# A Mamba-2 block on one core: decay matrices in steps of 64 tokens in place of 128

## The reference, cut to what matters

```python
proj = einsum('bsd,ed->bse', x, in_proj_w)          # gate | hBC | dt
hBC = silu(conv4(hBC))                              # hs | B | C
dt = clip(softplus(dt + dt_bias), 0, 100);  A = -exp(A_log)
xch = hs * dt                                       # in chunks of 128 tokens
A_cum = cumsum(dt * A)                              # in each chunk
L = exp(segsum(dt * A))                             # 128 x 128, lower triangle
Y_diag = einsum('lhn,shn,hls,shp->lhp', C, B, L, xch)
states = einsum('lhn,hl,lhp->hpn', B, exp(A_cum[-1] - A_cum), xch)
Y_off = einsum('lhn,hpn,hl->lhp', C, prev_states, exp(A_cum))
y = Y_diag + Y_off + hs * D;  g = y * silu(gate)
out = rmsnorm_per_group(g) * norm_w @ out_proj_w.T
```

## Time and profile before

| | |
|---|---|
| median of 3 runs | 1868.56 us (1868.19 to 1874.12) |
| profiled execution | 1870.32 us, span 1868.5 us |
| PE busy | 1754.7 us, 94% |
| PE weight loads | 1344.0 us, 72% |
| DVE busy | 1290.5 us, 69% |
| ACT busy | 1065.5 us, 57% |
| POOL busy | 942.1 us, 50% |
| mean granted TensorE clock | 0.988 |
| a group of four units | 216.9 us |

### The profile page before, as it was taken

The page is one execution under the profiler, slowest core; times in us unless marked ns, Lnnn a source line. Parts: engine busy times, 40 slices in busy tenths (PEclk is TensorE's granted clock), DMA queues, the critical chain, the costliest instruction groups (busy, mean ns, idle before and its releaser), DMA issues.

```text
span 1868.5 us, 31134 instructions
## 1 busy us (share of the span) xinstructions
PE 1754.7 (94%) x9656; PEld 1344.0 (72%) x9656; DVE 1290.5 (69%) x2095; ACT 1065.5 (57%) x1946; POOL 942.1 (50%) x721
## 2 busy tenths in 40 slices
PE   6799999999999999999999999999999999999966
PEld 5567777777777777777777777777777777777755
DVE  5766667666766677766676667666777666766788
ACT  6566555656646565665546566465656555565632
POOL 2355453556535464554535555355644545455563
PEclk9899999999999999999999999999999999999988
DMA  6412121111202121121211212121211212111121
GB/s 224 130 30 69 55 66 44 50 60 57 66 28 72 49 66 51 35 66 55 66 45 48 62 54 68 29 72 45 70 51 29 72 55 66 44 48 61 34 96 57
DMA packets 77097, 114.14 MB, mean 61 GB/s; under 512 B 21376, under 2 KB 28032, under 8 KB 76032
## 3 DMA queue, kind: packets, MB, share of 16 engines
q1 hardware_dynamic: 59360, 80.06, 14.2%
q10 hardware_dynamic: 17568, 31.99, 5.1%
HBM read 88.94 MB, written 23.07 MB: 60 GB/s over the span
## 4 chain that ended last, share of the span: by engine, by line
issue 46%; POOL 34%; PE 9%; DVE 5%; ACT 3%; DMA 1%; SPq 1%; POOLq 1%; ACTq 0%; DVEq 0%
POOL yt L1605 9%; POOL ssq L1600 7%; POOL wg_lo L1524 4%; POOL wo_lo L1524 4%; POOL prev L1586 3%; POOL yt L1608 3%; POOL wx_lo L1524 3%; PE bank L476 2%; PE bank L478 2%; PE bank L477 2%; PE bank L641 1%; PE bank L706 1%; DMA raw_w<-w_in_dram 1%; PE bank L840 1%; ACT lm L1072 0%
## 5 line engine op out<-in xcount | busy, mean ns | idle before, releaser
L1605 POOL TENSOR_TENSOR yt<-yt,ea 128x384 f32<-128x384 f32 (+1 forms) x128 | 189.6, 1481 | 393.1 <-DVE ea L1440 393.1
L1218 DVE SCALAR_TENSOR_TENSOR xc<-bank,bpar,xc 128x511 f32<-128x511 f32 (+2 forms) x384 | 285.4, 743 | 52.8 <-ACT xc L906 48.3
L1410 DVE TENSOR_TENSOR lm<-lm,cbm 128x512 f32<-128x512 f32 x256 | 185.9, 767 | 155.7 <-ACT lm L1075 155.7
L476 PE MATMUL bank<-h_hi,wg_hi 128*128 128x512 f32 x640 | 262.0, 409 | 31.3 <-ACT gate L1030 21.9
L478 PE MATMUL bank<-h_hi,wg_lo 128*128 128x512 f32 x640 | 251.0, 392 | 0.0
L477 PE MATMUL bank<-h_lo,wg_hi 128*128 128x512 f32 x640 | 250.2, 391 | 0.0
L476 PE MATMUL bank<-wo_hi,g_hi 128*128 128x512 f32 x496 | 206.9, 417 | 7.2 <-POOL wo_lo L1524 7.2
L476 PE MATMUL bank<-h_hi,wx_hi 128*128 128x512 f32 x512 | 210.3, 411 | 2.2 <-DVE bt L1218 2.2
L1586 POOL TENSOR_TENSOR prev<-prev,dec 128x512 f32<-128x512 f32 x96 | 102.0, 1063 | 206.0 <-DVE prev L1356 131.9
L478 PE MATMUL bank<-h_hi,wx_lo 128*128 128x512 f32 x512 | 200.3, 391 | 0.0
L477 PE MATMUL bank<-h_lo,wx_hi 128*128 128x512 f32 x512 | 199.9, 390 | 0.0
(11 more groups left out here) (187 smaller groups left out, 3796.9 us busy)
## 6 DMA issues: line engine op xcount, KB each, us to landing
raw_w<-w_in_dram SPq DMA_DIRECT2D x145, 256.0 KB, 2.6
raw_w<-w_out_dram SPq DMA_DIRECT2D x64, 256.0 KB, 2.6
part_d<-part ACTq DMA_DIRECT2D x64, 256.0 KB, 2.0
part<-part_d ACTq DMA_DIRECT2D x58, 256.0 KB, 2.7
rt<-rows_d SPq DMA_DIRECT2D x256, 8.0 KB
acc<-x_dram SPq DMA_DIRECT2D x8, 256.0 KB, 6.6
acc<-w_mod_dram SPq DMA_DIRECT2D x2, 1024.0 KB, 6.0
lh<-neg_d SPq DMA_DIRECT2D x128, 8.0 KB
```

The source lines that it names most:

```text
L476: nc.tensor.matmul(out_ap, whi(k), hhi(k), start=(k == 0), stop=False)
L1218: stt(dst[:, at], ps[:, 0:HALF - 3 + k], w(k), dst[:, at], ALU.mult, ALU.add)\
L1410: tt(lm[:, h % 4, :], lm[:, h % 4, :], cbm[:, toks(hf)], ALU.mult).then_inc(v_m, 1)
L1605: tt(yt[:, j % 2, cols], yt[:, j % 2, cols], ea[:, j % 2, cols], ALU.add).then_inc(p_t3, 1)
```

## The change

Steps of 64 tokens (`SUB`), two to a chunk of 128, for everything that has a decay in it.

- Differences, decays and mix: the matrix of a head is now 64 by 64 for each of 8 sub-chunks, packed with the even sub-chunks of a half on rows 0 to 63 and the odd ones on rows 64 to 127, two heads side by side in 512 columns. `diff(j)` is two products of 256 columns into bank 2; ACT has one Relu and one Exp a step for two, DVE one multiply for two. `lm` has two buffers for four.
- Y_diag: for each chunk four products of 64 rows, 64 weight columns and 64 columns, (head, sub-chunk) = (0, 0), (1, 1), (1, 0), (0, 1), with the two sub-chunks in two banks (3 and 5). The pass over `yt` is split in two. A semaphore increment of its own, `t_open`, stands ahead of them.
- Y_off: one matmul of 64 columns for each sub-chunk, k from 1 in even units.
- States: `states(z)` makes two products of 64 rows, into banks 6 and 7 (in odd units the last has one). 8 adds and 7 decays in an even unit, 7 and 7 in an odd one, for 4 and 3, and 3 and 3. `xw` is made for all four z in odd units too.
- Order on PE in the first part: `states(z-1)` follows the transposes of z and precedes the large product; in z = 3 come `states(2)`, `exp_a(0)`, `diff(0)`, `out_proj(2)`, `states(3)`, `out_proj(3)`. The waits for the last accumulate's variance and for B's transposes move to `states(0)`.
- Order on POOL: the group's rstd, decay 0, the splits of z = 0 and 1, decays 1 and 2, the splits of z = 2, the other decays, the splits of z = 3.
- Parameters: 12 DMAs into `rt`, 4 into `lh`, one into `dec`.
- Prologue: the sum restarts every 64 tokens (`seg`); one DVE pass and one exponential replace the 8 exponentials.

```diff
                 def states(z):
-                    te.wait_ge(v_xw, sb0 + z + 1)
...
+                    te.wait_ge(v_xw, 4 * u + z + 1)
...
                     else:
-                        te.wait_ge(v_prev, sb0 + z)
-                    nc.tensor.matmul(bank[7][:, :], bt[:, toks(hf, z, 1)], xw[:, z % 2, :],
-                                     start=True, stop=True).then_inc(t_st, 1)
+                        te.wait_ge(v_prev, ab0 + 2 * z)
+                    for s in range(1 if hf == 1 and z == NZ - 1 else 2):
+                        lst = nc.tensor.matmul(bank[6 + s][:, :], bt[sub_rows(s), toks(hf, z, 1)],
+                                               xw[sub_rows(s), z % 2, :], start=True, stop=True)
+                    lst.then_inc(t_st, 1)
...
+                def diff(j):
...
+                        te.wait_ge(a_fall, 4 * u + j)
+                    for i in range(2):
+                        lst = nc.tensor.matmul(bank[2][:, i * NZ * SUB:(i + 1) * NZ * SUB],
+                                               lh[par_][32 * j:32 * j + SROWS, i * 128:(i + 1) * 128],
+                                               rt[par_][32 * j:32 * j + SROWS, 0:NZ * SUB], start=True, stop=True)
+                    lst.then_inc(t_diff, 1)
...
+                    elif z == 1:
+                        ge(te, v_t2, 4 * u)
...
                 for z in range(NZ):
                     transposes(z)
+                    if z >= 1:
+                        states(z - 1)
                     if z == 2:
                         gate_proj(g, c, 3)
-                        states(1)
                         continue
                     if z == 3:
+                        exp_a(0)
+                        diff(0)
                         if not first and not end:
                             out_proj(u - 1, 2)
-                        states(2)
-                        exp_a(0)
-                        diff(0)
-                        diff(1)
+                        states(3)
...
-                    for z in range(1 - hf, NZ):
-                        lst = nc.tensor.matmul(bank[6][:, chunk(z)], prev[:, slot(hf, z), j * 128:(j + 1) * 128],
-                                               ct[:, toks(hf, z, 1)], start=True, stop=True)
+                    for k in range(1 - hf, NS):
+                        lst = nc.tensor.matmul(bank[6][:, k * SUB:(k + 1) * SUB],
+                                               prev[:, slot(k), j * 128:(j + 1) * 128],
+                                               ct[:, subtoks(hf, k)], start=True, stop=True)
                     lst.then_inc(t_yo, 1)
...
+                    te.sem_inc(t_open, 1)
                     for z in range(NZ):
-                        for i in range(2):
-                            h = 2 * j + i
-                            lst = nc.tensor.matmul(bank[5][64 * i:64 * i + 64, chunk(z)],
-                                                   xdt[:, z, h * HDIM:(h + 1) * HDIM], lm[:, h % 4, chunk(z)],
-                                                   start=True, stop=True)
+                        for i, s in ((0, 0), (1, 1), (1, 0), (0, 1)):
+                            h, at = 2 * j + i, (i * NZ + z) * SUB
+                            lst = nc.tensor.matmul(yd[64 * i:64 * i + 64, s, z * SUB:(z + 1) * SUB],
+                                                   xdt[sub_rows(s), z, h * HDIM:(h + 1) * HDIM],
+                                                   lm[sub_rows(s), j % 2, at:at + SUB], start=True, stop=True)
                     lst.then_inc(t_yd, 1)
...
+                def decay(k):
+
+                    if k == 1 - hf:
+                        po.wait_ge(d_par[hf], 272 * (nb + 1))
+                        ge(po, t_yo, 4 * u)
+                    po.wait_ge(v_prev, ab0 + k)
...
+                if not first and c in (0, 3):
+                    group_rstd(g - 1 if c == 0 else g, 1 if c == 0 else 0)
+                if hf == 1:
+                    decay(0)
+                for f in todo[0] + todo[1]:
+                    unit_fill(f, g)
+                decay(1)
+                decay(2)
+                for f in todo[2]:
+                    unit_fill(f, g)
+                for k in range(3, NS - hf):
+                    decay(k)
+                for f in todo[3]:
+                    unit_fill(f, g)
```

More of the change, by code:

```diff
@@ L47, in adaln_mamba_ffn @@
         xw = sb("xw", [128, 2, BLOCK])
[L48 to L49 removed]
+        prev = sb("prev", [128, NS, BLOCK])
+        lm = sb("lm", [128, 2, HALF])
         ea = sb("ea", [128, 2, HALF])
@@ L327, in _ @@
             xt = x.rearrange("(t p) n -> t p n", p=128)
-            mods = [flat(xdt, 0, 4), flat(gate, 0, 4), flat(prev, 0, 4), flat(lm, 0, 4), flat(acc, 0, 4), flat(acc, 4, 8)]
+            mods = [flat(xdt, 0, 4), flat(gate, 0, 4), flat(prev, 0, 4), flat(prev, 4, 8), flat(acc, 0, 4), flat(acc, 4, 8)]
             def load_mod(v):
@@ L501, in mod_row @@
                 te.wait_ge(d_mod[v], 16)
-                t, k0 = ((xdt, 0), (gate, 0), (prev, 0), (lm, 0), (acc, 0), (acc, 4))[v]
+                t, k0 = ((xdt, 0), (gate, 0), (prev, 0), (prev, 4), (acc, 0), (acc, 4))[v]
                 for k in range(NK):
@@ L679, in group_bc @@
                     for h2 in range(2):
[L680 to L683, removed]
+                        for k in range(NS):
+                            at = (h2 * NZ + k // 2) * SUB
+                            lst = nc.tensor.matmul(bank[2][sub_rows(k % 2), at:at + SUB], bt[:, subtoks(h2, k)],
+                                                   ct[:, subtoks(h2, k)], start=True, stop=True)
+                    lst.then_inc(t_cb, 1)
                     if first:
@@ L970, in _ @@
             keep_row(3)
-            se.wait_ge(v_scan, 2)
-            for z in range(NT):
-                lst = act(ea[:, z // 4, chunk(z % 4)], xw[:, z // 4, chunk(z % 4)], ACT.Exp, scale=-1.0,
-                          bias=xw[:, z // 4, (z % 4 + 1) * 128 - 1:(z % 4 + 1) * 128])
-            lst.then_inc(a_fe, 1)
+            se.wait_ge(v_drop, 1)
+            act(flat(ea, 0, 2), flat(ea, 0, 2), ACT.Exp).then_inc(a_fe, 1)
             pro_split(5)
@@ L1418, in lower_g @@
                         ALU.mult, ALU.subtract).then_inc(v_lo, 1)
+                new_state(5)
                 mix(0)
-                mix(1)
+                if not first and not end:
+                    accumulate(u, g1, b1, h1, 2)
+                new_state(6)
+                if hf == 0:
+                    new_state(7)
                 if not first and not end:
                     accumulate(u, g1, b1, h1, 3)
-                if hf == 0:
-                    new_state(3)
-                cols = slice(0 if hf else CHUNK, HALF)
+                cols = slice(0 if hf else SUB, HALF)
+                sub_first = lambda t: t.rearrange("p (z s l) -> p s z l", s=2, l=SUB)
                 for j in range(NCT):
                     if j < NCT - 1:
-                        mix(2 * j + 2)
-                        mix(2 * j + 3)
+                        mix(j + 1)
                     ve.wait_ge(t_yd, 4 * u + j + 1)
```

238 lines of the change are left out of this document (117 added, 121 removed).

## The result

The changed kernel takes 2053.2 us (median of 4 runs, 2049.8 to 2054.0) against 1870.7 for the kernel before in the same session: ratio 1.097, 95% interval 1.0945 to 1.0996, slower by 182.5 us. The forecast was 2192 us, with a range of 2040 to 2285. The direction and the range held; the likeliest case was 139 us too long, and rival A (2040 us) is the one that came nearest.

What follows compares the result with a forecast made beforehand. The prediction took PE, busy 94% of the span, as the bound; PE's added records, tiling changes, waits and clock loss, less waits taken back, summed to +323 us, giving 2192 us, range 2040 to 2285.

Steps and rivals of the forecast that it cites:

- rival A: PE quadrants wholly independent, both fp32 halves included: `xdt` by `lm` -55 us, state products +14; 2040 us, chance 0.16.
- B by C: On PE, once a group, 32 records with half the weight columns for 16; priced at nothing.
- Terms 2 and 3: On PE, partial overlap: `xdt` by `lm` on quadrants +49 us (0 to 97); state products on row groups +62 us.
- Term 1: `prev` by `ct` on PE: 8 more records a step, spacing set by weight load rather than columns: +102 us.
- Term 4: Changing PE's tiling in and out at each of four steps a unit: +40 us (0 to 52).
- Term 6: New PE waits before state pairs, for state adds behind POOL's decays and weight splits: +80 us (30 to 130).
- Rival C: State chain covered because a split or DMA comes earlier, so new waits and clock loss go: 2098 us, chance 0.06.
- Term 7: PE's clock falling after seven stalls of 6.4 us, 2 us each: +14 us (0 to 28).
- Term 8: PE waits taken back, for `ea`, the accumulate and half of the gate's: -24 us (0 to -40).
- Rival D: Faster: `prev` by `ct` records of 64 columns cost only their own 0.053 us; 1804 us, chance 0.04.
- B: No overlap over row groups on PE: `xdt` by `lm` +108 us, state products +110; 2294 us, chance 0.10.
- E: No difference: the saved decays pay for everything on ACT's side, if PE weren't the bound; chance 0.02.

Runs made afterwards that it cites:

- runs 3 and 4: Changed kernel with half the records of `prev` by `ct` (wrong results): one 128-column product per sub-chunk pair, 1982.9 us; the same list with 64 columns each, 1978.2 us.
- run 5: Changed kernel with one state product over all 128 rows in place of two over 64 rows (wrong states): 2036.4 us.
- Run 1: Changed kernel with decay 1 ahead of the weight splits on POOL, and later decays moved ahead likewise: 2013.2 us.
- runs 7 and 8: Run 1 with decays 3 and 5 ahead of splits, 2013.2 us; then the first accumulate behind the first state add in c = 0 and 3, 1993.1 us.
- run 2: Changed kernel with the sixteen `xdt` by `lm` products ordered one quadrant after another instead of in turns: 2154.3 us.
- run 6: Changed kernel, still 64-token steps, with PE's order of the kernel before, large product ahead of state products: 2074.7 us.

## Why the prediction was right in part

The sum again, with what the traces and runs show.

| term | forecast us | measured us | from |
|---|---|---|---|
| 1 `prev` by `ct` | +102 | +108 | 0.85 x 64 + 0.84 x 64 |
| 2 `xdt` by `lm` | +49 | -52 | (0.62 - 1.03) x 128 |
| 3 state products | +62 | +14 | 0.86 in 16 odd units |
| 4 changes of tiling | +40 | +46 | (3 x 0.18 + 0.09 + 4 x 0.20) x 32 |
| 6 new waits | +80 | +87 | 89.3 - 2.1 |
| 7 clock | +14 | +19 | 38 us of work at half clock |
| 8 taken back | -24 | -31 | rows 2 against the list above |
| B by C (in 5, at nothing) | 0 | -6 | (1.09 - 1.78) x 8 groups |
| sum | +323 | +185 | 182.5 measured |

**Terms 2 and 3 failed, by one assumption:** "again only neighbours of different products overlap, since a product's two records share a quadrant", and for the states "the second and third overlap and the others don't". The runs show whole products side by side: a pair of state products takes the time of one, and sixteen quadrant products stream in 0.6 of what eight took. I had rival A with just these values and gave it 0.16. In `xdt` by `lm` I took the middle between two bounds that both lay above the truth; the lower end there, no change, wasn't a bound, and A's -55 should have been it. The two terms came out 149 us below their forecast, the others 11 us above it together. The range held because its lower end had been set at A's sum, with 13 us to spare; term 2 itself had the wrong sign and lay outside its own bounds, so the range held by A and not by the mechanism that was forecast. The Trainium skill, "TensorEngine Tiling (Array Packing)", Key Properties, says that tiles work independently, weight loads and matmuls in parallel; the traces agree, 0.015 us a record with the quadrants in turns for 0.042 one after another.

**Term 1 held:** the one-column row of the trace before gave 0.10 us a record, eight more records cost 0.85 us, and runs 3 and 4 show that the columns have next to no part in it. (The 0.10 contains a short first distance; the single starts are 0.112 us apart at 1, 64 and 128 columns alike.) The sign given for it, 16 records in 1.6 to 1.8 us, was below the prediction's own sum, 1.08 + 0.8, and the measured 1.93. The same page of the Trainium skill, Instruction Overhead, gives a matmul about 60 cycles of overhead; by an estimate from that figure a record of 64 columns would cost half of one of 128, and this term nothing. No run agrees.

**Term 4** held in its sum, not in its parts: it took 0.09 us for going in everywhere, where behind the transposes it is 0.2, and run 5 puts the whole at 40 us for the state pairs.

**Term 6 held in its places as well as in its sum.** Forecast were 1.05 twice in c = 0, 1.7 in c = 1, nothing in c = 2, 6.4 and 0.95 in c = 3; the trace has 0.91 and 0.82, 1.51 and 0.29, nothing, 7.12 and nothing. Run 1 shows the cause that was named. What stays without the splits was mis-sized: 55 us of waits, where the prediction leaves 21 (7 x 0.95 and c = 0's share) and run 1's expectation 30, because the third split, the chain of adds and decays and DVE's accumulates are next (runs 7 and 8). Rival C falls with the wait of 7.1 us.

**Term 7** held, a little undersized. At each of the seven long waits the clock goes to half, for 6.8 or 10.2 us, and PE works in 4 to 6.5 us of it: 38 us in all, of which half is lost, 19 us.

**Term 8:** ACT's relief did reach PE's wait for the gate, 21.9 to 9.9 us, about the half that was taken.

Of the other signs DVE and POOL came near (1311 and 1093 us busy for 1300 and 1080). ACT was 954 us busy for 910, and PE's busy time grew by 136 us where its list was to grow by 230 to 260, which is terms 2 and 3 again.

Rival D, faster, fell with runs 3 and 4; B with the state pair, whose four records take what two take, and with run 2; E with the result.

## What to carry to other kernels

A short float32 product on TensorE (here up to 128 columns) with full 128 by 128 weights costs by its records, about 0.11 us each, and not by its columns: cutting 128 columns into two of 64 takes 1.93 us for 1.08, whatever the arithmetic saved. Cutting both dimensions onto quadrants is the other way round, as products on different quadrants run beside one another if they alternate in the list (0.62 us a step for 1.03). Each change into a row tiling and back costs, 0.3 us in run 5, so small groups must be kept together. When a serial chain gets more and shorter links, look in every queue on it for work that stood harmlessly between the old links, above all work that waits for a load.

## What the runs showed of the hardware

- Two float32 products on different row halves take the time of one (1.06 us for either, with 0.20 us of tiling in it), though each is two records.
- Float32 records with 128 by 128 weights start 0.112 us apart at 1, 64 and 128 columns (`ssq` and `prev` by `ct` before, `prev` by `ct` after).
- The same 32 records on four quadrants take 0.62 us in turns (four together every 0.058 us) and 1.47 us one quadrant after another.
- The clock fell to its 1.2 GHz level in places that the length of a wait doesn't foretell. In run 1 the units c = 3 have the same pair of waits in every group; behind second waits of 2.89, 2.30 and 2.46 us the clock was at half for 6.8 us, while 2.29, 2.53, 2.49 and 3.11 us left it at 1.00. In run 6 it fell at 1014.9 us, in front of the stretch shown above, with no longer wait of PE than 0.38 us in the 10 us before.
